# Experts with features on the partitions: copying each tile's up-projection weights to a fixed place instead of turning the product

## The reference, cut to what matters

```
x = x + _L0_xcond_ref(_layernorm(x), ...)          # the block
x = x + _L0_ffn_ref(_layernorm(x), wqkv, w1, w2)   # the experts
...
# E = 8 experts, F = 352 hidden features, H = 128, top 2 of 8 per token
x_rep = x[token_ids]                               # 2 * 8192 rows
for e in range(E):
    h1 = x_rep @ w1[e].T                           # 128 -> 2 * 352
    a, g = jnp.split(h1, 2, axis=-1)
    he = jax.nn.silu(a) * g @ w2[e].T              # 352 -> 128
    out = out + jnp.where((expert_ids == e)[:, None], he, 0)
out = out * scores.reshape(-1, 1)
combined = out.reshape(N, TOP_K, h).sum(axis=1)
```

## Time and profile before

| | us |
|---|---|
| median of 3 runs | 2274.69 (2274.27 to 2274.7) |
| the profiled execution | 2251.97 |
| its span, first to last instruction | 2250.1 |
| PE busy | 2105.5 |
| ACT busy | 1289.2 |
| DVE busy | 1263.8 |
| POOL busy | 822.7 |
| mean granted clock of PE, share of full | 0.983 |

### The profile page before, as it was taken

The page is one execution under the profiler, slowest core; times in us unless marked ns, Lnnn a source line. Parts: engine busy times, 40 slices in busy tenths (PEclk is TensorE's granted clock), DMA queues, the critical chain, the costliest instruction groups (busy, mean ns, idle before and its releaser), DMA issues. The chain is left out here.

```text
span 2250.1 us, 36649 instructions
## 1 busy us (share of the span) xinstructions
PE 2105.5 (94%) x10284; PEld 1280.5 (57%) x10285; DVE 1263.8 (56%) x3230; ACT 1289.2 (57%) x2456; POOL 822.7 (37%) x1022
## 2 busy tenths in 40 slices
PE   4899999999999999999999999999999788799996
PEld 3455555555555555555555555555555456577775
DVE  3454556575656565656565666656644734445454
ACT  3565666666656666656666666666655534444432
POOL 1122223333333334242433342424232434546654
PEclk8999999999999999999999999999999999999998
DMA  4001111111111111111212111121113111112265
GB/s 139 24 24 48 47 33 48 43 48 43 47 47 47 43 47 43 47 52 41 58 33 56 43 47 52 38 52 38 47 47 106 36 55 47 51 47 66 63 206 171
DMA packets 134430, 127.73 MB, mean 57 GB/s; under 512 B 14649, under 2 KB 108377, under 8 KB 134298
## 3 DMA queue, kind: packets, MB, share of 16 engines
q1 hardware_dynamic: 125018, 108.03, 17.3%
q0 software_dynamic: 9280, 18.28, 2.4%
HBM read 86.63 MB, written 40.67 MB: 57 GB/s over the span
## 5 line engine op out<-in xcount | busy, mean ns | idle before, releaser
L1721 POOL TENSOR_TENSOR pr<-pr,sm 128x512 f32<-128x512 f32 x256 | 262.8, 1045 | 760.2 <-DVE sm L1310 760.2
L732 PE MATMUL ps<-tt,V 128*128 128x512 f32 x1024 | 501.7, 594 | 4.5 <-ACT tt L1035 4.5
L1035 ACT ACTIVATE kp<-ps 128x512 f32<-128x512 f32 x512 | 295.8, 600 | 198.6 <-PE ps L269 195.2
L1300 DVE TENSOR_REDUCE mx<-ps 128x8 f32<-128x512 f32 x256 | 176.9, 691 | 335.2 <-PE ps L689 332.0
L689 PE MATMUL ps<-kp,hf 128*64 128x256 f32 x2048 | 279.3, 395 | 11.7 <-DVE pr L1303 8.7
L269 PE MATMUL ps<-hk,M 128*128 128x512 f32 x768 | 250.5, 450 | 27.2 <-DVE pr L1303 25.1
L1035 ACT ACTIVATE tt<-ps 128x512 f32<-128x512 f32 x512 | 273.6, 588 | 2.2 <-PE ps L719 2.2
L269 PE MATMUL ps<-cT,M 128*128 128x512 f32 x768 | 268.5, 473 | 0.0
L689 PEld LDWEIGHTS ps<-kp,hf 128*64 128x64 f32 x2048 | 125.5, 137 | 202.5 <-DVE pr L1303 130.2
L1035 ACT ACTIVATE pt<-ps 128x512 f32<-128x512 f32 x256 | 153.5, 600 | 151.8 <-PE ps L701 151.8
L1063 ACT ACTIVATE pr<-pr 128x512 f32<-128x512 f32 x256 | 161.7, 631 | 136.4 <-DVE pr L1303 134.7
(11 more groups left out here) (221 smaller groups left out, 3047.9 us busy)
## 6 DMA issues: line engine op xcount, KB each, us to landing
mod<-emb_s SPq DMA_DIRECT2D x96, 256.0 KB, 4.2
xr<-rows_s SPq DMA_DIRECT2D x144, 66.0 KB
cb<-y_s SPq DMA_DIRECT2D x32, 256.0 KB, 4.0
x_in<-in_x_dram SPq DMA_DIRECT2D x16, 256.0 KB, 4.4
xn_s<-x_in SPq DMA_DIRECT2D x16, 256.0 KB, 2.0
res<-xn_s SPq DMA_DIRECT2D x16, 256.0 KB, 2.7
c_in<-in_ctx_dram SPq DMA_DIRECT2D x16, 256.0 KB, 4.8
y_s<-res SPq DMA_DIRECT2D x16, 256.0 KB, 2.0
```

Of the source, the lines that this page charges most:

```text
L732: mm = nc.tensor.matmul(psO[:], Vw[a][:, g * HG + head_at(h), :], tt[:, h, :], start=(g == 0 and h == 0), stop=(g == 1 and h == HG - 1))
L1035: return nc.scalar.activation(o, i, ACT.Copy)
L1300: nc.vector.tensor_reduce(mx[:, p % 2, :], heads(psS[p % 2][:]), AX_X, ALU.max).then_inc(max_done, 1)
L1721: tensor(v, v, sm[:, p, :].unsqueeze(2).broadcast_to([P, HG, 64]), ALU.mult).then_inc(prob_done, 1)
```

## The change

In the new kernel the up-projection leaves the features on the partitions. The weights become the stationary operand and xT the moving one, in blocks of 128, 128 and 96 features (FK), for a and for g. The product ux is then already what the down-projection needs as its stationary operand, so turn_u and copy_u, their semaphores, one PSUM bank and the zeroed pads go. Before each tile the expert's columns for a are copied by ACT (copy_a) and those for g by DVE (copy_g) from WE to one of two fixed places (wt), so ACT and DVE fetch the tiles' places into registers themselves (places_of), a body or a unit at a time. PE's order within step n becomes turn_x(n+1), up(n), down(n-1); ACT's copy_x(n+1), copy_a(n+1), silu(n), weigh_y(n-1); DVE's copy_g(n+1), gate_mul(n). POOL's and SP's programs are the same. Silu and product work on 384 columns (128 tokens for each of the three blocks).

```diff
-            sl = sbb("sl", [P, 2, F])
+            sl = sbb("sl", [P, 2, 3 * P])
+            wt = sbb("wt", [P, 2, 2 * F])
             ux = sbb("ux", [P, 2, 3 * P])
-            uT = sbb("uT", [P, 2, 3 * P])
...
+        FK = [(k, min(P, F - k * P)) for k in range(3)]
...
-            def up(n, r, v):
+            def up(n, r):
+                pe.wait_ge(wa_cp, n + 1)
+                pe.wait_ge(wg_cp, n + 1)
                 pe.wait_ge(xt_cp, n + 1)
...
-                nc.tensor.matmul(bA[b][:, 0:F], xT[:, r % 2, :], WEf[:, bass.ds(v, F)], start=True, stop=True)
-                nc.tensor.matmul(bG[b][:, 0:F], xT[:, r % 2, :], WEf[:, bass.ds(v + F, F)], start=True, stop=True).then_inc(up_pe, 1)
-
-            def turn_u(n, r):
+                for bank, at in ((bA[b], 0), (bG[b], F)):
+                    for k, w in FK:
+                        mm = nc.tensor.matmul(bank[0:w, k * P:(k + 1) * P], wt[:, r % 2, at + k * P:at + k * P + w], xT[:, r % 2, :], start=True, stop=True)
+                mm.then_inc(up_pe, 1)
+
+            def down(n, r, v):
                 pe.wait_ge(u_done2, n + 1)
                 if not first(n):
-                    pe.wait_ge(ut_cp, n)
-                for k in range(3):
-                    mm = nc.tensor.transpose(bU[:, k * P:(k + 1) * P], ux[:, r % 2, k * P:(k + 1) * P], ident[:])
-                mm.then_inc(ut_pe, 1)
-
-            def down(n, r, v):
-                pe.wait_ge(ut_cp, n + 1)
-                if not first(n):
                     pe.wait_ge(y_cp, n)
-                for k in range(3):
-                    mm = nc.tensor.matmul(bY[:, 0:D], uT[:, r % 2, k * P:(k + 1) * P], WEf[:, bass.ds(v + 2 * F + k * P, P)],
+                for k, w in FK:
+                    mm = nc.tensor.matmul(bY[:, 0:D], ux[0:w, r % 2, k * P:(k + 1) * P], WEf[0:w, bass.ds(v + 2 * F + k * P, P)],
                                           start=k == 0, stop=k == 2)
                 mm.then_inc(y_pe, 1)
...
-                up(n, r, vs[k])
                 if nth_next is not None:
                     turn_x(n + 1, (r + 1) % TB, nth_next)
+                up(n, r)
                 if not (first(n0) and k < 1):
-                    turn_u(n - 1, (r - 1) % TB)
-                if not (first(n0) and k < 2):
-                    down(n - 2, (r - 2) % TB, vs[k - 2] if k >= 2 else earlier[k])
+                    down(n - 1, (r - 1) % TB, vs[k - 1] if k else earlier)
...
+            def copy_a(n, r, reg):
+
+                if not (isinstance(n, int) and n < 2):
+                    act.wait_ge(up_pe, n - 1)
+                v = act.snap(reg, donate=True, min_val=0, max_val=(E - 1) * WS)
+                copy(wt[:, r % 2, 0:F], WEf[:, bass.ds(v, F)]).then_inc(wa_cp, 1)
...
+            def step_act(n, r, nth, reg):
+                if reg is not None:
                     copy_x(n + 1, r + 1)
+                    copy_a(n + 1, r + 1, reg)
                 silu(n, r)
-                if not (isinstance(n, int) and n < 2):
-                    weigh_y(n - 2, (r - 2) % TB, nth)
+                if not first(n):
+                    weigh_y(n - 1, (r - 1) % TB, nth)
...
             def gate_mul(n, r):
                 dve.wait_ge(sil_done, n + 1)
                 if not (isinstance(n, int) and n < 2):
-                    dve.wait_ge(ut_pe, n - 1)
-                tensor(ux[:, r % 2, 0:F], bG[pair(n) if isinstance(n, int) else r % 2][:, 0:F], sl[:, r % 2, :], ALU.mult).then_inc(u_done2, 1)
-
-            def copy_u(n, r):
-                dve.wait_ge(ut_pe, n + 1)
+                    dve.wait_ge(y_pe, n - 1)
+                tensor(ux[:, r % 2, :], bG[pair(n) if isinstance(n, int) else r % 2][:, 0:3 * P], sl[:, r % 2, :], ALU.mult).then_inc(u_done2, 1)
+
+            def places_of(n0, count):
+
+                regs = [dve.alloc_register(f"v{next(serial)}") for r in range(count)]
+                for k in range(0, count, 4):
+                    m = min(4, count - k)
+                    dve.reg_load(regs[k:k + m], wtab[0:1, bass.ds(n0 + k, m)] if not isinstance(n0, int) else wtab[0:1, n0 + k:n0 + k + m])
+                return regs
+
+            def copy_g(n, r, reg):
+
                 if not (isinstance(n, int) and n < 2):
-                    dve.wait_ge(y_pe, n - 1)
-                nc.vector.tensor_copy(uT[:, r % 2, :], bU[:, 0:3 * P]).then_inc(ut_cp, 1)
+                    dve.wait_ge(up_pe, n - 1)
+                v = dve.snap(reg, donate=True, min_val=0, max_val=(E - 1) * WS)
+                nc.vector.tensor_copy(wt[:, r % 2, F:2 * F], WEf[:, bass.ds(v + F, F)]).then_inc(wg_cp, 1)
...
-                if isinstance(i, int) and (i, u) == (NC, 3):
-                    dve.wait_ge(eu_act, 3 * E)
-                    nc.vector.memset(WE[F - 2 * P:, :, 2 * F + 2 * P:WS], 0.0).then_inc(w_pad, 1)
-                    dve.wait_ge(s_done, 32 * NC)
-                    nc.vector.memset(ux[:, :, F:3 * P], 0.0).then_inc(w_pad, 1)
...
-            def tiles_dve(d, b=None):
+            def tiles_dve(d, b=None, last=False):
+                regs = places_of(TB * d + 1, TB - last)
                 for r in range(TB):
                     n = TB * d + r
-                    copy_u(n - 1, r - 1)
+                    if not (last and r == TB - 1):
+                        copy_g(n + 1, r + 1, regs[r])
                     gate_mul(n, r)
```

More of the change, by code:

```diff
@@ L273, in f32 @@
             return ap.bitcast(F32)
+        FK = [(k, min(P, F - k * P)) for k in range(3)]
+        assert sum(w for k, w in FK) == F
+        WEf = WE[:].rearrange("p e f -> p (e f)")
         SR = [psum[i] for i in range(4)]
@@ L811, in expert_turn @@
                 mm.then_inc(eu_pe, 1)
-            WEf = WE[:].rearrange("p e f -> p (e f)")
-            bA, bG, bX, bU, bY = (psum[3], psum[0]), (psum[4], psum[1]), psum[5], psum[6], psum[7]
-            kept = [pe.alloc_register(f"kept{r}") for r in range(2)]
+            bA, bG, bX, bY = (psum[3], psum[0]), (psum[4], psum[1]), psum[5], psum[7]
+            kept = pe.alloc_register("kept")
             def expert(reg):
@@ L861, in open_tiles @@
                 vs = [expert(reg) for reg in regs]
-                earlier = None if first(n0) else [pe.snap(kept[k], min_val=0, max_val=(E - 1) * WS) for k in range(2)]
+                earlier = None if first(n0) else pe.snap(kept, min_val=0, max_val=(E - 1) * WS)
                 return regs, vs, earlier
@@ L866, in close_tiles @@
                 regs, vs, _ = opened
-                for k in range(2):
-                    pe.reg_mov(kept[k], vs[len(vs) - 2 + k])
+                pe.reg_mov(kept, vs[-1])
                 for reg in regs:
@@ L889, in tiles_pe @@
                 if last:
-                    turn_u(TILES - 1, TB - 1)
-                    for k in (2, 1):
-                        down(TILES - k, TB - k, opened[1][TB - k])
+                    down(TILES - 1, TB - 1, opened[1][TB - 1])
                 close_tiles(opened)
@@ L1176, in copy_x @@
                 copy(xT[:, r % 2, :], bX[:, 0:P]).then_inc(xt_cp, 1)
+            def places_of(n0, count):
+                regs = [act.alloc_register(f"a{next(serial)}") for r in range(count)]
+                for k in range(0, count, 4):
+                    m = min(4, count - k)
+                    act.reg_load(regs[k:k + m], wtab[0:1, bass.ds(n0 + k, m)] if not isinstance(n0, int) else wtab[0:1, n0 + k:n0 + k + m])
+                return regs
[4 more added lines that the diff above has]
+                copy(wt[:, r % 2, 0:F], WEf[:, bass.ds(v, F)]).then_inc(wa_cp, 1)
             def silu(n, r):
@@ L1181, in silu @@
                     act.wait_ge(u_done2, n - 1)
-                nc.scalar.activation(sl[:, r % 2, :], bA[pair(n) if isinstance(n, int) else r % 2][:, 0:F], ACT.Silu).then_inc(sil_done, 1)
+                nc.scalar.activation(sl[:, r % 2, :], bA[pair(n) if isinstance(n, int) else r % 2][:, 0:3 * P], ACT.Silu).then_inc(sil_done, 1)
             def weigh_y(n, r, nth):
@@ L1209, in slot @@
                 li, lu = before(i, u)
+                opened = []
                 for p in range(NT):
@@ L1246, in slot @@
                     out_attn(li - 1, 1)
-                fill(i, u, HG)
+                fill(i, u, HG, opened)
+                for reg in opened:
+                    act.free_register(reg)
             ln_hi(0, 0)
@@ L1619, in slot @@
                     for n in tiles_at(i, u, h):
-                        tile_dve(n)
+                        n0 = tiles_before(i, u, 0)
+                        if n == n0:
+                            opened += places_of(n0 + 1, tiles_before(*after(i, u), 0) - n0)
+                        tile_dve(n, opened[n - n0])
+                for reg in opened:
+                    dve.free_register(reg)
                 if isinstance(i, int) and (i, u) == (NC, 1):
@@ L1650, in tiles_dve @@
                         combine(r - TB + 3, b + 1, 3 * b + r - TB + 4)
+                for reg in regs:
+                    dve.free_register(reg)
```

(20 more changed lines are left out.)

52 lines of the change are left out of this document (37 added, 15 removed).

## The result

| | before | after |
|---|---|---|
| median of 8 runs each, us | 2274.69 (2272.95 to 2277.4) | 2268.1 (2260.89 to 2272.28) |
| the profiled execution, us | 2251.97 | 2267.99 |
| its span, us | 2250.1 | 2266.2 |

The ratio is 0.9969, with a 95% interval of 0.9957 to 0.9981: 6.6 us faster, where 20.0 were forecast (2254.7, range 2246 to 2267). The time lies just above the range. The two profiled executions are the wrong way round, after above before.

A forecast was written before the change was run, and what follows sets the result against it. The prediction took the tile loop to be bound by PE. Its terms, -13.6 - 5.4 + 1.0 + 1.0 - 1.0 - 2.0 = -20.0 us, came off the median of 2274.69: 2254.7, range 2246 to 2267.

The forecast's parts named there:

- the base: Profiled execution 22.7 us below the median; this difference was assumed to carry over, so the gain was subtracted from 2274.69.
- ACT's and DVE's part: Added copies and fetches in tile bodies and unit openings: mostly covered, +1.0 us in all, between 0 and 9.
- threaded tiles: 64 tiles run among the block's last rounds: 32 follow PE's pace and gain 0.17 each, 5.4 us.
- lone tiles: The other 80 tiles, running alone and bound by PE: 0.17 us less each, 13.6 us.
- start: First tile: ACT fetches a register and copies before the first up, two tiles lack cover: +1.0 us (0 to 2).
- end: From the last up's end to the last scatter: 3.6 us instead of 5.6, so -2.0.
- The tile: PE's work per tile: turn 0.11, up 1.34 as twelve records, down 0.67; 2.12 us, 0.17 less than before.
- rival (c): PE's narrow matmuls bound by instruction issue: each tile loses 0.37 us, 41 slower, about 2313; chance 0.07.
- I cost them at nothing: Some 17 threaded tiles with only one pair of up banks free: no gain, between -0.1 and +0.2 us each.
- The seam's -1.0: Between the two tile groups: an earlier scatter and a body hole no longer adding to a late product, -1.0 us.
- (a): Rival: threaded tiles give nothing and each opening costs, 9 us in all; -6.6, so 2268; chance 0.12.
- (b): Rival: DVE and POOL hold each other off, delaying DVE's copy in bodies with adds; 12 us, so 2267; chance 0.10.

The follow-up runs named there:

- sessions 4 and 5: Changed kernel, unchanged, against the kernel before: 2237.18 us for 2254.36 without the stalls (ratio 0.9927), then 2268.35 for 2276.33 with them (0.9977).
- session 1: The result's own session, with the stalls: changed kernel against the kernel before, 2268.1 us for 2274.69, ratio 0.9969.
- session 4: Without the stalls: changed kernel against the kernel before, 2237.18 us for 2254.36, ratio 0.9927; with one fetch per tile 2228.85, ratio 0.9889.
- Single fetches: Changed kernel with ACT and DVE fetching one place before each tile's weight copy: ratio 0.9889 and 0.994 of the kernel before.
- session 6: With the stalls: changed kernel with one fetch per tile and SyncE's chunk loads issued later, against the kernel before: 2255.4 us, ratio 0.991.
- session 2: Changed kernel with one fetch per tile, against the kernel before at 2280.44 us by its rerun's measurement: 2262.97 us, ratio 0.994.

## Why the prediction was wrong, by its own steps

Two steps failed. One is the base that the sum was taken from, which cost 9 to 11 of the 13.4 us that the forecast was off. The other is a term of the sum, the 1.0 for ACT's and DVE's part, which should have been 11 or 12. Most of its error doesn't show in the total, because the threaded tiles gave 6 to 8 us more than forecast. That was luck.

**The base.** "The difference carries over" was said of the 22.7 us between the profiled execution and the median. It doesn't. The profile was of an execution without the stalls, the median of runs with them. They cost the kernel before 2276.3 - 2254.4 = 22 us and the changed one 2268.35 - 2237.18 = 31, by sessions 4 and 5. So 9 us of the gain go there (10.6 if the 6.6 of session 1 is set against session 4's 17.2). Why more of it falls on the changed kernel isn't shown. Most of the difference lies in the threaded tiles and the bodies with adds, not where the stalls are longest. That the changed kernel waits for ACT and DVE sooner behind each of PE's steps, with less work queued to go on with, is only a guess.

**The sum, where it was made for.** In session 4 the change gave 17.2 us for 20.0 forecast, inside the forecast's spread, but by terms that err both ways (profile against profile, 18.0):

| term | forecast | measured, session 4 |
|---|---|---|
| lone tiles, with fetches and seam | about -14 | -3.2 |
| threaded tiles, with fetches | about -5 | -13.3 |
| start (turn 0 to up 0: 0.89 and 1.60) | +1.0 | +0.7 |
| end (up 143 to last scatter: 6.76 and 4.94) | -2.0 | -1.8 |
| behind the last scatter | 0 | -0.6 |

- *The tile.* "0.11 + 1.34 + 0.67 = 2.12": 2.11 was measured. The records of the narrow matmuls stay 0.11 apart, and rival (c) is refuted. It decided nothing.
- *The lone tiles* hold the term that failed: "80 x 0.17 = 13.6" with "1.0 in all" for the fetches and DVE's adds. A plain body should take 8 x 2.12 + 0.60 = 17.6. Bodies 72 to 104 take 18.1 to 18.6, the first 19.24. Single fetches bring 17.6 to 17.95, so the fetches are what was missing, at 0.77 us a body (92.77 - 88.93 over five). In the four bodies with adds the mean is 19.65. There the fetches take 0.57, SyncE's loads 0.53 (the 74.20 of session 6), and some 0.7 over a plain body of 17.8 is left, DVE's adds and the seam among it. These shares are from single profiles and rough, as the same bodies take 78.22 with single fetches in session 2. The term should have been +3.8 for the plain bodies and some 2.0 for each of the four with adds, 12 in all and not 1.0. Taken from the table's first line it is 11.4 (-3.2 + 13.6 + 1.0). It lay beyond its upper bound of 9, half a microsecond for each opening, for which no row was given. The trace of before had the price. PE's hole of 2.35 at a unit's opening is three loads of 1.01, 1.01 and 0.30 us from a place that isn't a multiple of 4, while its loads in the bodies, from 8d, take 0.33. ACT's and DVE's fetches stand at 8d + 1, in front of copies that PE now waits for.
- *The threaded tiles.* "I cost them at nothing" was wrong for those on a single pair. They were 3.15 apart, with PE idle for 0.60. The timeline of session 4 has them 2.83 apart:

```profile
1881.87 1.56 PE L843 MATMUL ps<-xT,wt 128*128 128x128 f32 x12 [0.48 <-ACT xT L1030]
...
1884.70 1.57 PE L843 MATMUL ps<-xT,wt 128*128 128x128 f32 x12 [0.48 <-DVE ux L1592]
```

  Silu now follows up without the copy of x in between, and that returns more than up's growth takes. From up(10) to up(28), where nearly all are of this kind, it is 73.03 us for 77.90: 4.9 gained (3, if two further profiles of the kernel before with 76.0 are taken). The other 46 gave 8.4, or 0.18 each, where only 32 had been counted. That tiles which wait for something else now and then give their share too is a reading of this number; no run tests it.
- *Start and end* came as worked out. The seam's -1.0 can't be told from the bodies around it: the body there takes 19.52 for 21.46, of which 8 x 0.17 is the tiles' own.

**The rivals.** (a) names the time that was measured, 2268, but not the cause: the threaded tiles gave most of the gain. Only its openings did cost. (b) had the right effect in the wrong size. In the bodies with adds of session 4, 32 copies take 0.33 to 0.39 us, none near 1. But over the whole span the six copies above 0.42 (0.46 to 0.77, and one of 1.63) all overlap an instruction of POOL, those that overlap none take 0.35 at most, and seven of POOL's nine scatters above 1.1 overlap an add. The mean of 350 ns hides it, and it decides nothing here. The copy is nearer to what the Trainium skill has under *VectorE: DVE Perf Modes*, "Mode 2x_2P" (an estimate of 0.25 was made from it), than to the 0.5 taken.

**What stays open.** How a write to rows_s by an indirect DMA delays what other engines learn of PE, or PE itself, why it does so in whole sessions and not in others, and why the scatters to y_s, one per tile, don't. Also whether fetching from a multiple of 4 gives what single fetches give.

## What to carry to other kernels

Before a sum is set against a median, see that the profiled execution belongs to it: a profile 1% off its own median may lack something that the timed runs have, and a gain can differ between the two by more than its own error. Where a change lets the bounding engine wait for engines that used to be cover, count what those do at a loop's start as path, register fetches above all. Look in the trace at what a fetch costs from the place where it will stand, and spread the fetches over the iterations or move them to a cheaper place. And when one wait at a loop's start is taken away, look which queue is next: here a fix was worth nothing before the other and 2 us or more after it.

## What the runs showed of the hardware

- A fetch of four places from SBUF into registers takes mostly 0.31 to 0.37 us if the first place is a multiple of 4, and 0.9 to 1.1, now and then up to 1.6, from any other, on PE, ACT and DVE alike. One place takes mostly 0.28 to 0.31. Two fetches of four at 8d + 1 leave ACT idle for 2.3 us.
- In some sessions, at indirect DMAs to one buffer, PE's semaphore increments stand 4 to 5 us behind the records of their matmuls instead of 0.3 to 0.5. PE, idle in the meantime, is then granted 0.50 of its clock. This costs 22 us in one kernel and 31 in another that does the same DMAs.
- DVE copies 352 fp32 columns inside SBUF in 0.35 us where ACT takes 0.50. Copies that overlap no instruction of POOL take 0.35 at most, a few that do up to 0.77, and one 1.63.
- Six fp32 matmuls of 128 moving columns with 128 or 96 weight columns, new weights for each, are twelve records 0.11 us apart, with the weight loads beside them.
